# A residual sum moved from VectorE into PSUM: attention's output added to X by products with the identity

## The reference, cut to what matters

```
def _L1_xattn_ref(target, source, target_mask, source_mask, Wq, bq, Wk, bk, Wv, bv):
    ...
    q = jnp.einsum('oc,bct->bot', Wq, target) + bq[None, :, None]
    ...
    dot = jnp.einsum('bhdt,bhds->bhts', q, k) / math.sqrt(HEAD_DIM)
    ...
    amap = jax.nn.softmax(dot, axis=-1) * mask
    out = jnp.einsum('bhts,bhds->bhdt', amap, v)
    return out.reshape(b, HEADS * HEAD_DIM, t)
...
x = x + jnp.tanh(g_xattn[1]) * _L1_xattn_ref(_layernorm(x, axis=-1), ctx_2048, ...)
x = x + jnp.tanh(g_ffn[1]) * _L1_ffn_ref(_layernorm(x, axis=-1), ...)
```

## Time and profile before

| | |
|---|---|
| median of 3 runs | 511.44 us (511.41 to 511.58) |
| profiled execution | 511.55 us |
| its span in the profile | 509.8 us |
| busy in the span | PE 474.0, DVE 380.9, ACT 245.1, POOL 230.5 us |
| PE's granted clock, 200 to 350 us | 1.00 |

### The profile page before, as it was taken

One profiled execution on the slowest core, in us unless ns is written; L12 is line 12 of the kernel. 1 busy time (PEld: TensorE's weight loads), 2 busy tenths in 40 slices (PEclk: granted clock), 3 DMA queues, 4 the chain that ended last, 5 costly groups with the idle time before them and its releaser, 6 DMA issues. The chain is left out here.

```text
span 509.8 us, 10287 instructions
## 1 busy us (share of the span) xinstructions
PE 474.0 (93%) x3384; PEld 259.0 (51%) x3384; DVE 380.9 (75%) x765; ACT 245.1 (48%) x461; POOL 230.5 (45%) x319
## 2 busy tenths in 40 slices
PE   2999999998999989999999999898999999999993
PEld 2663664754733533333344333333445647788882
DVE  4979889899888779999999999998555624333321
ACT  2751232322232078899999998777512001233331
POOL 3727433155656454867767763213010560042433
PEclk9999999999999999999999999999999999999998
DMA  7750086002675216566666665300022225378843
GB/s 237 213 175 0 16 186 95 2 0 62 181 195 141 66 43 177 148 167 175 165 172 163 179 159 147 82 5 6 1 81 90 74 94 166 120 178 201 193 111 41
DMA packets 67256, 59.96 MB, mean 118 GB/s; under 512 B 10048, under 2 KB 62256, under 8 KB 67216
## 3 DMA queue, kind: packets, MB, share of 16 engines
q1 hardware_dynamic: 63712, 55.24, 39.5%
q0 software_dynamic: 3072, 4.21, 4.9%
q10 hardware_dynamic: 432, 0.00, 0.0%
HBM read 38.90 MB, written 22.50 MB: 120 GB/s over the span
## 5 line engine op out<-in xcount | busy, mean ns | idle before, releaser
L1308 DVE TENSOR_REDUCE MX<-psum 128x2 f32<-128x512 f32 x256 | 162.2, 683 | 9.9 <-PE psum L1173 8.4
L1357 ACT ACTIVATE HP<-psum 128x512 f32<-128x512 f32 x224 | 122.4, 601 | 29.2 <-PE psum L1188 26.8
L1173 PE MATMUL psum<-QKA 60*128 60x256 bf16 x512 | 81.4, 273 | 7.3 <-DVE MX L1308 5.9
L1188 PE MATMUL psum<-QKA 60*128 60x256 bf16 x512 | 81.2, 273 | 1.6 <-DMA QKA<-max_scr 1.1
L1274 PE MATMUL psum<-HP,VP 128*32 128x256 f32 x1024 | 81.8, 391 | 0.3 <-issue 0.2
L588 PE MATMUL psum<-space_a,space_w 128*128 128x512 f32 x160 | 73.1, 601 | 2.8 <-DVE HP L615 2.0
L1173 PEld LDWEIGHTS psum<-QKA 60*128 60x128 bf16 x512 | 31.6, 94 | 64.2 <-DVE MX L1308 43.7
L1945 POOL DMA_INDIRECT out_x<-OE,to_u x16 | 24.9, 1558 | 62.7 <-ACT OE L1980 60.2
L588 PEld LDWEIGHTS psum<-space_a,space_w 128*128 128x128 f32 x160 | 29.0, 190 | 37.4 <-issue 31.9
L2068 PE MATMUL psum<-XT,WE 128*128 128x256 f32 (+1 forms) x192 | 44.0, 379 | 1.0 <-DVE HE L2234 1.0
L199 PE MATMUL psum<-space_a,wsh 128*128 128x512 f32 (+1 forms) x96 | 43.6, 598 | 0.3 <-PEq L1480 0.3
(11 more groups left out here) (203 smaller groups left out, 766.8 us busy)
## 6 DMA issues: line engine op xcount, KB each, us to landing
QKA<-stack_scr SPq DMA_DIRECT2D x32, 480.0 KB, 4.6
stack_scr<-PARTS SPq DMA_DIRECT2D x32, 192.0 KB, 2.1
WE<-in_W SPq DMA_DIRECT2D x16, 352.0 KB
stack_scr<-PARTS SPq DMA_DIRECT2D x32, 128.0 KB, 2.0
XD<-dispatched SPq DMA_DIRECT2D x8, 258.0 KB, 3.8
X<-in_x SPq DMA_DIRECT2D x4, 512.0 KB, 5.7
CTX<-in_ctx SPq DMA_DIRECT2D x4, 512.0 KB, 8.0
MB<-in_mask SPq DMA_DIRECT2D x16, 128.0 KB, 3.2
```

The source lines that it names most:

```text
L1173: return pe.matmul(to[:, tt * T:(tt + 1) * T], QKA[rows, k, 0, h, tt * P:(tt + 1) * P], QKA[rows, k, 1, h, :], start=True, stop=True)
L1188: return pe.matmul(to[:, (m % 2) * T:(m % 2 + 1) * T], QKA[rows, k, 1, h, st * P:(st + 1) * P], QKA[rows, k, 0, h, :], start=True, stop=True)
L1308: dve.tensor_reduce(MX[:, par, head_of(n), :], src[:, :].rearrange("p (a s) -> p a s", a=2), axis=AX.X, op=ALU.max).then_inc(a_red, 1)
L1357: act.activation(PT[:, i % 2, st, 2 * half:2 * half + 2, :].rearrange("p j t -> p (j t)"), TBK3[THIRDS[m]], ACT.Exp).then_inc(a_exp, 1)
```

## The change

PE's two transposes of YA become four products of 128x128 float32. For each half of the columns, a product of the identity and X's columns starts the sum in PSUM, and a product of YA and the identity is added to it. ACT then copies the result over X, and DVE's sum is gone. ACT has the copy at slot 5, behind that slot's exponentials. The waits on `a_x3` that PE had stay, and DVE gets three of its own before the statistics.

```
@@ -1285,9 +1285,12 @@
                 def pe_yo(pe, b):
+
                     pe.wait_ge(a_ya, b + 1)
                     for tt in range(2):
-                        last = pe.transpose(MISC[:, tt * P:(tt + 1) * P], YA[:, tt, :], ident[:])
+                        x = slice(tt * P, (tt + 1) * P)
+                        pe.matmul(MISC[:, x], ident[:], X[:, bass.ds(b, 1), x].rearrange("p b c -> p (b c)"), start=True, stop=False)
+                        last = pe.matmul(MISC[:, x], YA[:, tt, :], ident[:], start=False, stop=True)
                     last.then_inc(a_yo, 1)
@@ -1326,9 +1329,9 @@
-                def dve_x3(dve, b):
-                    dve.wait_ge(a_yo, b + 1)
-                    dve.tensor_tensor(xb(b), xb(b), MISC[:, 0:T], ALU.add).then_inc(a_x3, 1)
+                def act_x3(act, b):
+                    act.wait_ge(a_yo, b + 1)
+                    act.activation(xb(b), MISC[:, 0:T], ACT.Copy).then_inc(a_x3, 1)
@@ -1557,6 +1560,8 @@
                             if p == 0 and there(b, 1):
                                 act_nm(act, b + 1)
+                            if p == 5 and there(b, -1):
+                                act_x3(act, b - 1)
@@ -1763,9 +1768,9 @@
-                            if p == 5 and there(b, -1):
-                                dve_x3(dve, b - 1)
                             for t in STAT4.get(tail(b, p), ()):
+                                dve.wait_ge(a_x3, GB * (t + 1))
+                                alone(dve)
                                 dve_statistics(ln4, tiles_of(t))
```

## The result

The changed kernel takes 519.86 us (519.12 to 521.35, 5 runs) against 511.41 us (511.38 to 511.58, 5 runs): 1.0169 times as long, interval 1.0152 to 1.0186. The prediction was 519.1 us, with a range of 515 to 522. The profiled execution took 519.12 us with a span of 517.4, against 509.8 before: 7.6 us more. The granted clock of the attention part, 200 to 350 us, is 1.00 in both, so the clock is not the cause.

A forecast was written before the change was run, and what follows sets the result against it. It took PE's and DVE's paths, tied at score 14's reduce, as the bound; 5.8 (steps 2 to 9) + 0.2 (step 1) + 0.4 (10 to 13) + 1.3 (15 and 16) = 7.7 us gave 519.1 us, range 515.0 to 522.0.

The forecast's parts named there:

- Two paths arrive together: In a loop step, DVE's and PE's paths reach score 14's reduce together, so removing DVE's 0.33 us sum gains nothing.
- The products hold PE 0.67 longer: Four products before tiled work hold PE 1.04 us where two transposes held it 0.37, in each step.
- the register step adds 0.06: In steps 2 to 9, addressing X by a register puts 0.06 us a step on PE's path, bounds 0 and 0.12.
- Steps 10 to 13 at 0.09 each: Without a query product, score 12 has 0.58 us of slack against 0.67, so 0.09 us is lost per step.
- Step 14 hidden in a transfer's wait: Step 14's 0.67 us goes into PE's wait of 1.09 for the key maxima's transfer and costs 0.
- steps 15 and 16 at 0.67: In the last two steps no reduces are left and PE is the bound: 0.67 us each, 1.3 in all.
- ACT's copy at 0.48, no wait of the query product: ACT's copy at slot 5 takes 0.48 us, is covered, and ends 0.6 us before the query product needs X.
- No new wait at the end: At the attention's end, products and copy move PE and DVE both by about 0.7 us, and PE stays last.
- products as cheap as transposes: Rival: the products cost PE only 0.22 us more a step, giving 512.3 us; chance 0.06.
- ACT becomes the bound: Rival: ACT's copy comes late and the query product waits for it, giving 523.1 us; chance 0.05.
- Part of the delay is made up inside the step: Rival: slack between score 14 and the next YA cuts a loop step's cost to 0.40 us, 516.5 us; chance 0.17.
- the loop's 5.8: Steps 2 to 9 lose 0.73 us each, from products and register step, all on the path: 5.8 us.

The follow-up runs named there:

- e1: The changed kernel with the two transposes back, ACT copying their result over X and no sum: 509.47 us.
- e7: The kernel before, with ACT copying the result to its own tile and GpSimd adding it to X in steps 1 to 13: 509.43 us.
- e5: The kernel before with the query product moved from ahead of score 14 to between scores 14 and 15: 510.52 us.
- e8: e7 with the query product moved as in e5, to between scores 14 and 15: 506.84 us.
- e2: The changed kernel with DVE instead of ACT copying the products' result over X: 519.15 us.
- e3: The kernel before with YA's two transposes made as two plain products, DVE's sum kept: 513.20 us.
- e4: The changed kernel with the products' X taken from a fixed sequence, so without a register step on PE: 519.94 us.
- e6: The changed kernel with the query product moved from ahead of score 14 to between scores 14 and 15: 517.18 us.

## Why the prediction was right

- **Two paths arrive together, and DVE's relief is worthless in the loop.** Shown, to within 0.1 us: e1 and e7 gain 0.07 a step for 0.33, e5 gains 0.08 for 0.66, e8 gains 0.34 for both. The tie was not exact; PE's path was the later one in the loop. The four reduces of step 6 take 2.56, those of step 10, which has no query product, 2.47, and so do those of e5, where score 14 comes early. So DVE stood some 0.09 in that run of reduces, which the prediction read as one without a gap, and that is e5's 0.08.

  "Worthless" was 0.07 too strong, because PE's path held a wait for DVE's sum. The prediction took the query product's start as PE's own time, but it waits for X with `a_x3`. Step 5 of the kernel before, then step 6 of e1:

```profile
246.50 0.60 DVE L1323 SCALAR_TENSOR_TENSOR YA<-psum,maskG,RD 128x128 f32<-128x128 f32 x2
...
248.08 0.64 PE L1274 MATMUL psum<-HP,VP 128*32 128x256 f32 x8
...
248.22 0.41 DVE L1331 TENSOR_TENSOR X<-X,psum 128x256 f32 x1
...
248.75 0.69 PE L674 MATMUL psum<-Z,wq 128*128 128x256 f32 x2
```

```profile
259.12 0.64 PE L1274 MATMUL psum<-HP,VP 128*32 128x256 f32 x8
...
259.69 0.70 PE L674 MATMUL psum<-Z,wq 128*128 128x256 f32 x2
```

In the kernel before the query product starts 0.67 behind the value products in step 5 and 0.60 in step 6, but in every step of the loop 1.65 or 1.66 behind YA's end, just after DVE's sum. In e1 and e7 it starts 0.57 behind the value products in every step, and score 14 comes 0.03 to 0.11 earlier, step by step what the step gains. In the loop the profile names no releaser for it, so there the starts alone show the wait; in step 1 of the kernel before it names DVE's sum:

```profile
201.96 0.30 PEld L674 LDWEIGHTS psum<-Z,wq 128*128 128x128 f32 x2 [0.44 <-DVE X L1331]
```

- **The products hold PE 0.67 longer, and the register step adds 0.06.** The cause is shown by e2, e3 and e4. The sizes were off a little, in both directions. The hold was 1.08 for 1.04, and the start came 0.15 behind YA's end, 0.09 later than the transposes' 0.06, where 0.06 had been allowed for the register step; without the register it is 0.05 again (e4). From YA's end to score 12 it became 0.80 longer (0.43 to 1.23), against 0.73. But score 12 to score 14 became 0.12 shorter (1.86 to 1.74): with PE later, X is ready in time, and the query product's wait for it is gone (263.99 - 263.42 = 0.57 behind the value products). The prediction did not see this slack. In e3, which keeps DVE's sum but delays PE, the query product stands 0.57 behind the value products as well, and the same 0.28 - 0.12 = 0.16 comes out. So 0.69 a step was measured for 0.73: 5.54 for 5.8. DVE's gap before score 14 was 0.45, a little under the 0.5 to 0.7 that was to show it.
- **Steps 10 to 13 at 0.09 each.** They took 0.15. The slack of 0.58 was right; the products held PE 1.09 instead of 1.04, and so ate 0.05 more of it than the sum allowed.
- **Step 14 hidden in a transfer's wait, steps 15 and 16 at 0.67.** -0.03, +0.73 and +0.61. The wait in which step 14 hid shrank from 1.09 to 0.40, so 0.40 of cover is left.
- **ACT's copy at 0.48, no wait of the query product.** The copy took 0.384, less than the query's bias that it was read from, and the query product did not wait. e2 shows that ACT's hand-over costs nothing.
- **No new wait at the end.** As a statement on the profile it was wrong: DVE has two waits for X there, 1.82 and 2.13. As one on time it held, since PE is still the last, by 0.33.

Of the rivals, "products as cheap as transposes" falls with e3, "ACT becomes the bound" with e2. "Part of the delay is made up inside the step" is wrong at the place that it named, between score 14 and the next YA. The next YA of the kernel before and of the changed kernel:

```profile
269.74 0.60 DVE L1323 SCALAR_TENSOR_TENSOR YA<-psum,maskG,RD 128x128 f32<-128x128 f32 x2
```

```profile
273.36 0.60 DVE L1326 SCALAR_TENSOR_TENSOR YA<-psum,maskG,RD 128x128 f32<-128x128 f32 x2
```

From score 14 to it are 269.74 - 261.01 = 8.73 and 273.36 - 264.62 = 8.74: a delay of score 14 passes on undiminished, as the prediction said. What is made up, 0.12, lies ahead of score 14.

The sum, 7.7, met the 7.6 of the profiled execution. That it is so close is in part luck: the loop's 5.8 was 0.26 too high and the 0.4 of steps 10 to 13 was 0.19 too low. The median of five lies 0.7 higher than that execution, and this part no step of the prediction foresaw; of all seven executions of the changed kernel the middle one took 519.34.

## What to carry to other kernels

Where two engines meet at one event with both nearly full, relieving either alone gives almost nothing (here less than 0.1 us for 0.33 and for 0.66), and lengthening the later one costs nearly all of it (0.69 of 0.80; lengthening DVE's path was not tried). Find the event, work out both arrival times, and relieve both paths or neither. Follow each path through its waits for the other engine too: here PE's held one for DVE's sum. A wait of engine A for engine B in the waits' table does not make B the bound, as long as B waits for A elsewhere in the same step. Moving work out of a path helps only as far as the next event behind it: e6's query product left score 14 and held score 15.

## What the runs showed that was not expected

- A register-addressed operand on PE, a step of 46 ns in the trace, put off the start of the products by 0.10 us (0.15 against 0.05 behind YA's end), and it came to 0.09 us a loop step.
- Executions of the changed kernel are spread over 519.05 to 521.35 us, some 2.3 us, more than the 1.7 between all executions of the kernel before (510.96 to 512.69). In the profiled executions of e4 and e6, the part behind the attention is 1.7 to 1.9 us longer than in the changed kernel's. In e6 an idle time of PE stands there:

```profile
465.24 1.99 PE L2075 MATMUL psum<-XT,WE 128*128 128x256 f32 x8 [1.57 <-DMA WE<-in_W]
```

The expert layer waits 1.57 us for the weights of an expert. That this also makes the changed kernel's longer executions longer is only likely: none of them has a profile. In e4 the same group of products waits 1.40, and the profile puts it down to DVE's `HE` instead:

```profile
466.71 1.99 PE L2073 MATMUL psum<-XT,WE 128*128 128x256 f32 x8 [1.40 <-DVE HE L2239]
```

That `HE` was written at 466.20, but the changed kernel's trace has the same products running from 465.6, before its own `HE` of that place at 466.89, and by the kernel's text (`gu_expert`) they wait for the tokens, for the expert's weights and for an earlier `HE` only. The tokens were there at 464.21, so by exclusion the weights are what e4 waited for too. What makes the weights late in some executions stays open.
